# Attention hops of a graph network on one core: order of the steps, fills on TensorE and share of the last scaling

## What is computed

```python
def agg(x):
    a_input = jnp.concatenate([x[head], x[tail]], axis=-1)
    e = jnp.sum((a_input @ fc_w.T + fc_b) * rel_e, axis=-1)
    e = jnp.where(e > 0, e, 0.2 * e)
    m = jax.ops.segment_max(e, head, num_segments=N)
    ex = jnp.exp(e - m[head])
    w = ex / segment_sum(ex, head)[head]
    return segment_sum(x[tail] * w[:, None], head) + x
for _ in range(n_hops):          # 2
    x = agg(x)
    x = x / jnp.maximum(norm(x), 1e-12)
```

## Time and profile before

| what | us |
|---|---|
| median of 3 runs | 6409.13 (6401.49 to 6412.13) |
| the profiled execution, its own time | 6410.99 |
| span of the profiled execution | 6409.2 |
| hop one, first to last maximum (52 octets) | 3602.6 to 4424.6 |
| hop two, first to last maximum (52 octets) | 4473.0 to 5328.9 |

### The profile page before, as it was taken

The page is one execution under the profiler, slowest core; times in us unless marked ns, Lnnn a source line. Parts: engine busy times, 40 slices in busy tenths (PEclk is TensorE's granted clock), DMA queues, the critical chain, the costliest instruction groups (busy, mean ns, idle before and its releaser), DMA issues. The chain is left out here.

```text
span 6409.2 us, 146244 instructions
## 1 busy us (share of the span) xinstructions
PE 5644.9 (88%) x32700; PEld 4709.4 (73%) x32701; DVE 4652.7 (73%) x16722; ACT 4457.7 (70%) x15208; POOL 3534.5 (55%) x3365
## 2 busy tenths in 40 slices
PE   6537999987799999899999899997888887999999
PEld 2326999976677777699999677775666666888888
DVE  9986999987655552377777555555777776988898
ACT  1966999982244442288888577775999995777777
POOL 0776777757666667744444454444455554444444
PEclk9668999998899999999999899998999998999999
DMA  1045777768666666677777677776788874444443
GB/s 50 3 8 167 214 212 211 211 210 251 205 193 194 196 190 201 184 221 222 223 222 221 180 219 217 215 218 176 240 248 251 252 234 129 127 125 127 127 126 119
DMA packets 1164323, 1175.57 MB, mean 183 GB/s; under 512 B 307118, under 2 KB 1038421, under 8 KB 1163282
## 3 DMA queue, kind: packets, MB, share of 16 engines
q1 hardware_dynamic: 1012692, 956.04, 49.1%
q0 software_dynamic: 151360, 216.47, 13.6%
HBM read 963.01 MB, written 393.59 MB: 212 GB/s over the span
## 5 line engine op out<-in xcount | busy, mean ns | idle before, releaser
L215 POOL DMA_INDIRECT landing_first<-messages,by_dst_meta x768 | 826.4, 1076 | 665.2 <-PE l1b_ps_b L1578 368.2
L215 POOL DMA_INDIRECT landing_last<-x,by_dst_meta x384 | 434.9, 1133 | 569.4 <-PE l_ps_a L1715 484.9
L2022 POOL DMA_INDIRECT landing_last<-z,by_src_meta x408 | 425.4, 1043 | 433.3 <-PE l2b_ps_g L2272 309.0
L2022 POOL DMA_INDIRECT landing_last<-x,by_src_meta x408 | 409.9, 1005 | 405.9 <-PE l2a_ps_g L2272 243.1
L215 POOL DMA_INDIRECT landing_first<-in_x,by_src_meta x384 | 404.7, 1054 | 187.4 <-PE l_ps_a L1010 119.3
L1532 ACT ACTIVATE l1a_x_t<-l1a_ps_x,by_dst_first 128x256 f32<-128x256 f32 x400 | 168.0, 471 | 398.0 <-PE l1a_ps_x L1564 398.0
L1576 PE MATMUL l1b_ps_b<-root,l1b_x_t 128*128 128x256 f32 x1600 | 425.9, 389 | 0.0
L1576 PE MATMUL l1a_ps_b<-root,l1a_x_t 128*128 128x256 f32 x1584 | 416.4, 385 | 2.8 <-issue 1.3
L1020 PE MATMUL l_ps_b<-l_w,l_both 128*128 128x256 f32 x1624 | 418.0, 380 | 0.0
L1023 PE MATMUL l_ps_b<-l_w,l_agg_t 128*128 128x256 f32 x1624 | 416.8, 379 | 0.0
L1734 PE MATMUL l_ps_b<-l_w,l_mix_t 128*128 128x256 f32 x1592 | 396.5, 392 | 9.9 <-DVE l_mix_t L1651 9.8
(11 more groups left out here) (418 smaller groups left out, 18172.0 us busy)
## 6 DMA issues: line engine op xcount, KB each, us to landing
l_both<-in_x_both SPq DMA_DIRECT2D x416, 256.0 KB
z<-l2a_result SPq DMA_DIRECT2D x400, 152.0 KB
x<-l1b_result SPq DMA_DIRECT2D x392, 152.0 KB, 3.2
l2a_x<-x SPq DMA_DIRECT2D x48, 1216.0 KB
l1b_x<-h SPq DMA_DIRECT2D x408, 128.0 KB
l1b_res<-x SPq DMA_DIRECT2D x408, 128.0 KB
l1a_x<-x SPq DMA_DIRECT2D x404, 128.0 KB
l_x<-x SPq DMA_DIRECT2D x402, 128.0 KB, 2.3
```

Source lines behind the costliest of these rows:

```text
L215: pool.indirect_dma_start(gathered[:, slot, 0:D], None, source[0:count, :], bass.IndirectOffsetOnAxis(ap=rows, axis=0), bounds_check=limit ...
L2022: pool.indirect_dma_start(gathered[:, k, :], None, x_in[0:N_NODES, :], bass.IndirectOffsetOnAxis(ap=rows, axis=0), bounds_check=limit, oob ...
```

## The change

In hop one the root of an octet and its scaling are done one round later (`have_square`, `square`, `weigh`, `improve`, `guess` and `scale_rows` go from one ahead to none), and the last five squares stand behind the scaling. All 34 fills of hop one and 20 of the 24 of hop two go. In hop two the second aggregates stand ahead of `spread`, both halves of `add_self` ahead of `maximum`, `find_nodes` ahead of `maximum`, the squares ahead of both roots, and the scaling ahead of the copies; three of the eight last scalings go to VectorE, and the store waits on their semaphore. The rings keep two octets. `squares` becomes bf16, and `restart` is cut to the items behind the fixed octets.

```diff
+LATER = -(-MAX_ITEMS // RING) * RING + 3 * RING - OCTETS_FIXED * OCT
+SCALED_BY_DVE = 3
-        squares = ph.sb("squares", [P, OCT, D], F32)
-        restart = ph.sb("restart", [P, ITEMS], F32)
+        squares = ph.sb("squares", [P, OCT, D], BF16)
+        restart = ph.sb("restart", [P, LATER], F32)
...
-                        sp.wait_ge(s["out_ready"], octet.item + (q + 2))
+                        if last_hop and q < SCALED_BY_DVE:
+                            sp.wait_ge(s["scaled"], octet.number * SCALED_BY_DVE + (q + 1))
+                        elif last_hop:
+                            sp.wait_ge(s["out_ready"], octet.number * (OCT - SCALED_BY_DVE) + (q - SCALED_BY_DVE + 2))
+                        else:
+                            sp.wait_ge(s["out_ready"], octet.item + (q + 2))
...
+                def scale_some(o):
+                    o.wait(dve, norm.shifted)
+                    for j, k in o.each()[:SCALED_BY_DVE]:
+                        dve.tensor_scalar(result[:, k, :], result[:, k, :], inv2.root[:, k:k + 1], norm.bias[:, k:k + 1], ALU.mult, ALU.add)\
+                            .then_inc(s["scaled"], 1)
...
 # VectorE, hop two, then hop one
-                    steps = [(add_residual, 0), (centre, 0), (scores, 2), (guard, 1), (part(add_self, 0), 1), (part(add_up, 0), 1),
-                             (have_variance, 0), (maximum, 2), (part(add_self, 1), 1), (part(add_up, 1), 1), (find_nodes, 3),
-                             (have_square, 1), (lambda o: inv2.square(dve, o), 0), (lambda o: inv2.weigh(dve, o), 0),
-                             (lambda o: inv2.improve(dve, o), 0), (square, 1), (weigh, 1), (shift_bias, 0), (improve, 1)]
+                    steps = [(add_residual, 0), (guard, 1), (centre, 0), (scores, 2),
+                             (part(add_self, 0), 1), (part(add_up, 0), 1), (part(add_self, 1), 1), (part(add_up, 1), 1),
+                             (have_variance, 0), (find_nodes, 3), (maximum, 2), (have_square, 1),
+                             (lambda o: inv2.square(dve, o), 0), (lambda o: inv2.weigh(dve, o), 0),
+                             (lambda o: inv2.improve(dve, o), 0), (square, 1), (shift_bias, 0), (weigh, 1), (improve, 1),
+                             (scale_some, 0)]
-                    steps = [(find_nodes, 3), (scores, 2), (guard, 1), (part(add_self, 0), 1), (part(add_up, 0), 1), (maximum, 2),
-                             (part(add_self, 1), 1), (part(add_up, 1), 1), (have_square, 1), (square, 1), (weigh, 1), (improve, 1)]
+                    steps = [(find_nodes, 3), (guard, 1), (scores, 2), (part(add_self, 0), 1), (part(add_up, 0), 1),
+                             (maximum, 2), (part(add_self, 1), 1), (part(add_up, 1), 1), (have_square, 0), (square, 0),
+                             (weigh, 0), (improve, 0)]
 # ScalarE
-                    for j, k in o.each():
+                    for j, k in o.each()[SCALED_BY_DVE:]:
...
-                    steps = [(lambda o: norm.square(act, o, result), 0), (lambda o: measure(o, 0, 4), 1), (lambda o: inv2.guess(act, w.shift, o), 0),
-                             (part(chances, 0), 2), (part(chances, 1), 2), (lambda o: measure(o, 4, 4), 1), (decay, 2),
-                             (lambda o: inv.guess(act, w.shift, o), 1), (part(take_chances, 0), 2), (part(take_chances, 1), 2), (apply, 0)]
+                    steps = [(lambda o: norm.square(act, o, result), 0), (lambda o: measure(o, 0, 4), 1),
+                             (lambda o: measure(o, 4, 4), 1), (lambda o: inv2.guess(act, w.shift, o), 0),
+                             (lambda o: inv.guess(act, w.shift, o), 1), (part(chances, 0), 2), (part(chances, 1), 2), (decay, 2),
+                             (apply, 0), (part(take_chances, 0), 2), (part(take_chances, 1), 2)]
-                    steps = [(lambda o: measure(o, 0, 3), 1), (part(chances, 0), 2), (part(chances, 1), 2), (decay, 2),
-                             (part(take_chances, 0), 2), (lambda o: measure(o, 3, 5), 1), (part(take_chances, 1), 2),
-                             (lambda o: inv.guess(act, w.shift, o), 1), (part(scale_rows, 0), 1), (part(scale_rows, 1), 1)]
+                    steps = [(part(chances, 0), 2), (part(chances, 1), 2), (decay, 2), (part(take_chances, 0), 2),
+                             (lambda o: inv.guess(act, w.shift, o), 0), (lambda o: measure(o, 0, 3), 1),
+                             (part(take_chances, 1), 2), (part(scale_rows, 0), 0), (part(scale_rows, 1), 0),
+                             (lambda o: measure(o, 3, 5), 1)]
 # TensorE
-                    steps = [(part(aggregate, 0), 1), (part(aggregate, 1), 1), (part(aggregate, 2), 1), (spread, 2), (part(aggregate, 3), 1),
-                             (part(fill, 16), 2), (part(turn_chances, 0), 2), (look_up, 3), (part(fill, 4), 2),
-                             (part(turn_chances, 1), 2), (part(fill, 4), 2)]
+                    steps = [(part(aggregate, 0), 1), (part(aggregate, 1), 1), (part(aggregate, 2), 1), (part(aggregate, 3), 1),
+                             (spread, 2), (part(turn_chances, 0), 2), (look_up, 3), (part(turn_chances, 1), 2),
+                             (part(fill, 4), 2)]
-                    steps = [(part(aggregate, 0), 1), (part(aggregate, 1), 1), (part(fill_early, 4), 1), (spread, 2),
-                             (part(aggregate, 2), 1), (part(aggregate, 3), 1), (part(fill_late, 20), 1), (part(turn_chances, 0), 2),
-                             (part(fill_late, 4), 1), (part(turn_chances, 1), 2), (look_up, 3), (part(fill_late, 6), 1)]
+                    steps = [(part(aggregate, 0), 1), (part(aggregate, 1), 1), (part(aggregate, 2), 1), (spread, 2),
+                             (part(aggregate, 3), 1), (part(turn_chances, 0), 2), (look_up, 3), (part(turn_chances, 1), 2)]
```

More of the change, by code:

```diff
@@ L1036, in count_edges_and_message @@
     FAST_CHUNKS = FAST // P
-    COUNTED = -(-MAX_ITEMS // RING) * RING + 3 * RING - FAST
+    COUNTED = LATER
     SCANS_AT = R1 // 2
@@ L1905, in attention_hop @@
             "score", "e_done", "peak", "top", "wrapped", "old_top", "minus", "below", "empty", "shrunk", "chance", "p_turned", "made",
-            "agg_done", "mixed", "added", "guarded", "squared", "summed")}
+            "agg_done", "mixed", "added", "guarded", "squared", "summed",
+            "scaled")}
         s["stored"] = [ph.sem(f"stored{k}") for k in range(HOP)]
@@ L2135, in maximum @@
                     o.wait(dve, s["peak"])
-                    dve.tensor_tensor_scan(top[:, o.base + 1:o.base + 1 + OCT], restart[:, bass.ds(o.item, OCT)], peak[:, o.both],
+                    dve.tensor_tensor_scan(top[:, o.base + 1:o.base + 1 + OCT], restart[:, bass.ds(o.item - OCTETS_FIXED * OCT, OCT)], peak[:, o.both],
                                            top[:, o.base:o.base + 1], ALU.add, ALU.max).then_inc(s["top"], 1)
                     o.wait(dve, s["top"])
-                    dve.tensor_tensor(old_top[:], top[:, o.both], restart[:, bass.ds(o.item, OCT)], ALU.add)\
+                    dve.tensor_tensor(old_top[:], top[:, o.both], restart[:, bass.ds(o.item - OCTETS_FIXED * OCT, OCT)], ALU.add)\
                         .then_inc(s["old_top"], 1)
@@ L2179, in _ @@
                 dve.drain().then_inc(s["zeroed"], 1)
-                dve.tensor_scalar(restart[:], graph.keep[:], -2 * MASK, 2 * MASK, ALU.mult, ALU.add).then_inc(s["zeroed"], 1)
+                dve.tensor_scalar(restart[:], graph.keep[:, OCTETS_FIXED * OCT:OCTETS_FIXED * OCT + LATER], -2 * MASK, 2 * MASK, ALU.mult, ALU.add).then_inc(s["zeroed"], 1)
                 dve.wait_ge(s["zeroed"], 2)
@@ L2307, in fill @@
                     keep_busy(pe, c, ps_spare, n)
[L2309 to L2316, removed]
                 if last_hop:
-                    steps = [(part(aggregate, 0), 1), (part(aggregate, 1), 1), (part(aggregate, 2), 1), (spread, 2), (part(aggregate, 3), 1),
-                             (part(fill, 16), 2), (part(turn_chances, 0), 2), (look_up, 3), (part(fill, 4), 2),
-                             (part(turn_chances, 1), 2), (part(fill, 4), 2)]
-                else:
-                    steps = [(part(aggregate, 0), 1), (part(aggregate, 1), 1), (part(fill_early, 4), 1), (spread, 2),
-                             (part(aggregate, 2), 1), (part(aggregate, 3), 1), (part(fill_late, 20), 1), (part(turn_chances, 0), 2),
-                             (part(fill_late, 4), 1), (part(turn_chances, 1), 2), (look_up, 3), (part(fill_late, 6), 1)]
+                    steps = [(part(aggregate, 0), 1), (part(aggregate, 1), 1), (part(aggregate, 2), 1), (part(aggregate, 3), 1),
+                             (spread, 2), (part(turn_chances, 0), 2), (look_up, 3), (part(turn_chances, 1), 2),
+                             (part(fill, 4), 2)]
+                else:
+                    steps = [(part(aggregate, 0), 1), (part(aggregate, 1), 1), (part(aggregate, 2), 1), (spread, 2),
```

(1 more changed line is left out.)

## The result

The changed kernel takes 6456.81 us (median of 4 runs, 6452.73 to 6458.75) beside 6406.83 for the kernel before on the same chip: a ratio of 1.0077, interval 1.006 to 1.0095. The forecast was 6432, with 6340 to 6480 around it. The profiled execution of the changed kernel has a span of 6457.0 us where the one of before has 6409.2.

A forecast was written before the change was run, and what follows sets the result against it. Hop one was taken as bound by waits, hop two nearly by ScalarE. Rounds going from 16.12 to 16.3 (+9 us) and 16.7 to 17.0 (+14 us) gave 6434 profiled, 6432 median against 6409; range 6340 to 6480.

The forecast's parts named there:

- The wait for squares goes: Hop one: VectorE's 4.90 us wait for squares goes, as squares are done a round earlier.
- the gather ring: Hop one: aggregates, gathers, landing, scores, spread, last aggregates; 15.75 us before, 14.73 after, 15.1 with the mean's 0.37.
- the landing: Hop one: the stretch from the fourth gather to the scores, taken as 5.18 us.
- all high: Rival, both hops: the clock stays up, rounds of 15.1 and 15.2 us, 6289 us in all; chance 0.09.
- The clock falls once a round in both hops: Without fills TensorE idles in each round, so its granted clock falls to between 0.7 and 0.85.
- What it costs: Low clock: hop one +1.2 us a round, 15.1 to 16.3; hop two from 15.2 to 17.0.
- all low: Rival: the clock does not come up before the spread; rounds of 17.6 and 17.9 us, 6539 us; chance 0.07.
- Hop two is bound by ScalarE: Hop two: ScalarE's 15.9 us a round falls to 14.4 without three scalings; round 15.2 if TensorE is in time.
- a TensorE ring within one round: Hop two: turns, look-up, fills, aggregates, sums, node tests, maximum, roots, exponentials; 12.9 us, or 19.6 all at low clock.
- The gain of some 2 us a round that the new order offers: Both hops: the new order's gain, said to be eaten by the low clock.
- Three scalings on VectorE cost nothing: Hop two: at most 1.5 us more brings VectorE to 13.8 us a round, under 17.0, so no cost.
- Stores with two rounds to spare: Hop one: stores leave SyncE later, but loads of x queued behind them have two rounds to spare.

The follow-up runs named there:

- e1: The changed kernel with the fills put back in both hops, all else as changed: 6403.77 us, 1.0004 of the kernel before.
- e3: The changed kernel with all eight last scalings of hop two on ScalarE again: 6447.24 us, 1.0065 of the kernel before.
- e10: Hop one as changed with its fills back, hop two's old orders and fills, three scalings on VectorE; first chip: 6396.7 us, 0.9995 of the kernel before.
- e5: The changed kernel with fills back and hop two's stores ahead of the head loads, on the second chip: 6860.25 us, 1.0169 of the kernel before.
- e11: The kernel of e5 run again on the first chip: 6390.01 us, 0.9983 of the kernel before.
- e8: The kernel of e10 on the second chip: 6739.16 us, 0.9981 of the kernel before.
- e12: The kernel of e11 with hop two's node tests moved behind the roots, on the first chip: 6332.41 us, 0.9896 of the kernel before.
- e6: The kernel of e12 on the second chip: 6808.66 us, 1.0086 of the kernel before.
- e9: Hop one as changed with its fills back, hop two wholly as before, all eight scalings on ScalarE; first chip: 6382.61 us, 0.9975 of the kernel before.

## Why the prediction was right, and which of its steps failed

The time fell in the range and on the side forecast, 50 us slower where 23 were forecast, but the number is in part luck: two errors of opposite sign met in it. The low clock was priced too high in both hops, and the change of hop two with the clock up was put at a gain of 1.5 us a round where e1 shows a loss of 0.6. Hop one came out at 16.16 for the 16.3 of the sum, hop two at 17.82 for 17.0.

*The wait for squares goes; what is late next is the gather ring.* Right, as is the gain of 1.02 for the pair moved ahead of the spread. e1 has the ring without low clock: aggregates end 4031.05, first gather 4031.86, fourth 4035.77, `both` 4041.75, spread 4043.14 to 4045.37, last aggregates 4046.55. That is 0.81+3.91+5.98+1.39+2.23+1.18 = 15.50. **The term that was mis-sized is the landing**: 5.18 was taken over from the earlier trace rows, and it is 5.98. (Over the window of hop one its median is 5.3 us before and 5.9 in the changed kernel and in e1, so most of the 0.8 is no accident of the rounds shown.) The forecast 15.1 with all high became 15.63, so hop one offers 0.5 us and not 1.0. These are e1's rows, GpSimd and VectorE:
```profile
4035.77 1.00 POOL L2032 DMA_INDIRECT landing_last<-x,by_src_meta  x1 [0.30 <-issue]
```
```profile
4041.75 0.36 DVE L2089 TENSOR_TENSOR l2a_both<-l2a_ps_s,landing_last 128x192 f32<-128x192 f32 x1 [3.50 <-DMA landing_last<-x,by_src_meta]
```
Why the same gathers land later is open. In e1 the round moves as many bytes in less time (221 GB/s for 214, a DMA share of 0.73 for 0.71), but the changed kernel, at 214 and 0.71, has them as late, and no run isolates it.

*The clock falls once a round in both hops.* Right: 0.81 and 0.73, inside the 0.7 to 0.85 forecast, and slow look-ups in each round of hop two. *What it costs*: 1.2 was set for hop one, and fills or no fills make 0.53 (16.16 - 15.63). For hop two the sum had 1.8 (15.2 to 17.0), and they make 0.44 (17.82 - 17.38), though e1 has not the full clock there (0.88). Both terms were mis-sized, over twofold in hop one and fourfold in hop two. Why the low clock costs so little is argued, not shown: part of what runs slowly would have waited for landings anyway. The rival of all low has a slip besides: it takes 17.6 for hop one where the working gives 18.1. The Trainium skill, "TensorE: Matmul & The Clock Gate", section "Why this matters for your kernels", asks for short gaps between bursts. The trace agrees in direction: without the fills the gaps cost 47 us, and 109 in the old order. But the gaps of TensorE in hop one over the two rounds up to the one shown, 2.4 us at most, are shorter than those that the section warns of, and the clock fell all the same.

*Hop two is bound by ScalarE, 15.2 once three scalings leave.* **This step failed.** e1, at a clock of 0.88, takes 17.38, not 15.2; e3 and e10 show that ScalarE's load can go up by 60 us in the window without lengthening the round, and down by 74 without shortening it. The prediction walked a TensorE ring within one round (12.9 to 19.6) and had the node tests in it, but it closed that ring at the aggregates, and left out that eight gathers behind one block of aggregates take 9.3 us to issue and 5 to 6.5 more to land before the scores two octets on. That ring, with the node tests in it, is what sets the round. "The gain of some 2 us a round that the new order offers" was 0.5 in hop one, and -0.6 in hop two. With the clock up (all high) the forecast would have been 6289; the kernel with its fills back takes 6404.

*The order itself is not at fault, one entry of it is.* With the node tests behind the roots, hop two comes to 15.92, 0.86 under before: over half of the 1.5 that the prediction saw in the change of hop two (16.7 to 15.2).

*Three scalings on VectorE cost nothing.* Priced at 1.5 us at most for three, they take 1.05 to 1.2 (0.40 each, partly overlapped). That they cost nothing holds in the new order as far as the interval of e3 can tell, not in the old one, where they cost 14 us.

*Stores with two rounds to spare.* The prediction said so of the loads of x in hop one, and nothing there waits for them. It missed hop two: VectorE waited 42 us for the residual, whose loads queue behind the stores, and the place of the stores is worth 13 to 22 us.

## What to carry to other kernels

A ring that goes through a ring buffer of two takes two rounds: walk it from a result to the same result two octets on, through every queue, before calling an engine the bound; the fullest engine (ScalarE, 95%) wasn't it alone: relieved of three scalings, which VectorE took, the round did not get shorter. When work that feeds DMAs is put together in one block, the issues become one block too, and the last landing moves out by the whole length of issuing. Look for small operations in front of the one that others wait for: 1.5 us of node tests that a later place hides were worth 58 us, more than all the rest of the change.

## What had not been expected of the hardware

Chips can differ by more than any edit here: the kernel before takes 6400 us on two of those used and 6753 on a third, and orders don't keep their rank between them. e5 and e11 are one kernel: 1.0169 of before on the one, 0.9983 on the other. On the second chip hop two of it moves to 19.78 us a round from 17.24, while the old order goes only from 17.12 to 17.36 (e10 and e8). There is no profile of the kernel before from that chip, so why the new order suffers more there is not shown. On the best order: e12 is 0.9896 of the kernel before on the first chip, but the same kernel is 1.0086 on the second (e6). The safe part is hop one's order with its fills (e9 at 0.9975; e8, which has the three scalings too, at 0.9981).

A second finding is where the low clock shows: in hop one, after 2.13 us of idling, the next turn still took 0.66 us for its four matmuls, and the second one, behind the look-up, 1.09, with TensorE busy in between. In hop two, after 5.16 us, the first turn took 1.00 already. So in hop one what the edit costs is not seen at the idle stretch but in the work some steps behind it.
